# A query tile's projection moved from step 3 to step 2, and two bursts of value products placed later, in an attention kernel

## The reference

```python
xn = layer_norm(x, norm_w, norm_b)
q = (xn @ q_w + q_b).reshape(Bx, Tx, H, -1)
k = (xn @ k_w + k_b).reshape(Bx, Tx, H, -1)
att = jnp.einsum('bnhl,bmhl->bnmh', q, k)
att = jax.nn.softmax(att + (1.0 - mask) * -1000000.0, axis=2)
v = ((xn @ v_w + v_b) * src_mask[:, :, None]).reshape(Bx, Tx, H, -1)
y = jnp.einsum('bnmh,bmhl->bnhl', att, v).reshape(Bx, Tx, Dx)
```

## Time and profile before

| | us |
|---|---|
| median of three runs | 2839.5 (2839.39 to 2840.51) |
| the profiled execution | 2837.53 |
| its span, first to last instruction | 2835.7 |
| mean granted TensorE clock | 0.981 |

### The profile page before, as it was taken

How to read it: one execution, slowest core, us unless ns; L and a number is a source line. 1 busy time by engine, 2 the same in 40 slices (tenths; PEclk the granted TensorE clock), 3 DMA queues, 4 the chain that set the end, 5 groups by cost and what they waited for, 6 DMA issues and landing times. The chain is left out here.

```text
span 2835.7 us, 43874 instructions
## 1 busy us (share of the span) xinstructions
PE 2684.1 (95%) x13890; PEld 1951.8 (69%) x13890; DVE 1822.6 (64%) x3276; ACT 1228.2 (43%) x2040; POOL 1343.5 (47%) x598
## 2 busy tenths in 40 slices
PE   6899999999999999999999689999999999999997
PEld 3565566556655665566555468888888888888886
DVE  4666666666666666666665566777676677666673
ACT  2455555555555555555555423333333333333332
POOL 0365655655666565556566323433333333433332
PEclk9999999999999999999999799999999999999999
DMA  7555656665666566656654411111111111111100
GB/s 181 123 95 95 94 80 94 94 96 78 94 97 98 74 97 98 96 78 96 95 83 69 147 35 49 49 49 45 48 49 45 36 46 41 49 49 35 47 30 30
DMA packets 114915, 211.44 MB, mean 75 GB/s; under 512 B 12408, under 2 KB 14508, under 8 KB 114876
## 3 DMA queue, kind: packets, MB, share of 16 engines
q1 hardware_dynamic: 78012, 143.81, 21.7%
q10 hardware_dynamic: 36864, 67.13, 17.8%
HBM read 74.87 MB, written 34.18 MB: 38 GB/s over the span
## 5 line engine op out<-in xcount | busy, mean ns | idle before, releaser
L879 DVE TENSOR_REDUCE negmax<-max_bank 128x1 f32<-128x512 f32 x1024 | 684.5, 687 | 333.6 <-PE max_bank L506 329.4
L745 ACT ACTIVATE probs<-exp_bank 128x512 f32<-128x512 f32 x1024 | 591.9, 596 | 564.2 <-PE exp_bank L521 469.0
L284 POOL TENSOR_TENSOR probs_sum<-probs_sum,probs 128x2048 f32<-128x2048 f32 x126 | 580.6, 4608 | 86.2 <-ACT probs L745 83.8
L284 POOL TENSOR_TENSOR probs_sum<-probs 128x2048 f32<-128x2048 f32 x63 | 287.9, 4570 | 587.0 <-ACT probs L745 587.0
L506 PE MATMUL max_bank<-k_stack,q_stack 98*128 98x512 f32 x1024 | 426.6, 418 | 27.6 <-DVE negmax L879 22.8
L521 PE MATMUL exp_bank<-q_stack,k_stack 100*128 100x512 f32 x1024 | 422.5, 424 | 23.1 <-ACT probs L745 22.5
L506 PEld LDWEIGHTS max_bank<-k_stack,q_stack 98*128 98x128 f32 x1024 | 195.2, 191 | 149.0 <-issue 58.5
L521 PEld LDWEIGHTS exp_bank<-q_stack,k_stack 100*128 100x128 f32 x1024 | 193.6, 190 | 127.6 <-ACT probs L745 73.1
L1500 POOL TENSOR_TENSOR sT_lo<-silu,sT_hi 128x512 fp32r<-128x512 f32 x128 | 172.8, 1370 | 175.8 <-DVE sT_hi L1615 175.8
L532 PE MATMUL y_bank<-probs,v_sb 128*32 128x512 f32 x2048 | 247.7, 602 | 0.0
L1281 PE MATMUL b_work<-ident,area 128*128 128x128 f32 x1536 | 192.8, 281 | 23.8 <-DMA b_sums<-sums_scratch 12.0
(11 more groups left out here) (203 smaller groups left out, 5308.6 us busy)
## 6 DMA issues: line engine op xcount, KB each, us to landing
q_stack<-q_stage ACTq DMA_DIRECT2D x128, 256.0 KB
k_stack<-k_stage ACTq DMA_DIRECT2D x128, 256.0 KB
x_sb<-in_x SPq DMA_DIRECT2D x16, 1024.0 KB, 5.4
q_stack<-q_stage SPq DMA_DIRECT2D x64, 256.0 KB
k_stack<-k_stage SPq DMA_DIRECT2D x64, 256.0 KB
yT_scratch<-y_stage SPq DMA_DIRECT2D x64, 256.0 KB
area<-yT_scratch SPq DMA_DIRECT2D x16, 1024.0 KB, 5.3
area<-in_x SPq DMA_DIRECT2D x64, 256.0 KB, 2.8
```

The costliest lines, as they stand in the source:

```text
L284: eng.tensor_tensor(probs_sum[:, :, :], so_far, probs[:, mt, :, :], ALU.add).then_inc(probs_added, 1)
L745: act.activation(probs[:, mt, j, :], exp_bank[k % 2][:, :], ACT.Exp).then_inc(exp_done, 1)
L879: dve.tensor_reduce(negmax[:, m:m + 1], max_bank[m % 2][:, :], AXX, ALU.max, negate=True).then_inc(max_done, 1)
```

## The change

Four things are altered.

- The tables `QUARTERS` and the rules in `uses_of` become one table `TILES`: for each step, each tile, its group, and the slots of its quarters. The q tile of group 1 of the next row moves from step 3 (slots 0 to 3) to step 2 (named q', slots 8 to 11). The k tile of group 1 stays in step 3, with its quarters in slots 0, 2, 4, 6 in place of 4 to 7. The other tiles keep their slots.
- The first burst and ACT's copy of y stand with exponential 6 in place of 5 (slot 9), in all steps.
- The second burst stands with exponential 10 (slot 13) in steps 1 and 2; in steps 0 and 3 it stays with exponential 8.
- The semaphores of the stacks are kept apart for q and k, so that a wait for one does not count the copies of the other; SP's low part of q' stands behind the shift rows of step 2.

```diff
-        stack_in = [sem(f"stack_in{g}") for g in range(NG)]
+        stack_in = {n: [sem(f"{n}_stack_in{g}") for g in range(NG)] for n in "qk"}
...
+        def tiles_of(g, last):
+            return {n: t for n, t in TILES[g].items() if not last or g == 0 or (g == 1 and n in "qk")}
+
         def uses_of(g, last):
...
+            at = [(slots[0], n) for n, (_, slots) in tiles_of(g, last).items()]
             if g == 1 and not last:
+                at += [(k, f"x{tt}") for tt, k in enumerate(X_TURNS)]
             if not last or g < NG - 1:
+                at.append((MAX_TURN, "m"))
+            return [n for _, n in sorted(at)]
+
+        TILES = [
+            {"q": (2, (0, 1, 2, 3)), "k": (2, (4, 5, 6, 7)), "v2": (2, (8, 9, 10, 11)), "v3": (3, (13, 14, 15, 15))},
+            {"q": (3, (0, 1, 2, 3)), "k": (3, (4, 5, 6, 7))},
+            {"q": (0, (0, 1, 2, 3)), "k": (0, (4, 5, 6, 7)), "q'": (1, (8, 9, 10, 11))},
+            {"k": (1, (0, 2, 4, 6)), "v0": (0, (8, 9, 10, 11)), "v1": (1, (13, 14, 15, 15))},
+        ]
+        X_TURNS = (8, 9, 11, 13)
+        MAX_TURN = 12
+        SECOND_BURST = (8, 10, 10, 8)
...
-        QUARTERS = {"q": (0, 1, 2, 3), "k": (4, 5, 6, 7), "v": (8, 9, 10, 11), "v'": (13, 14, 15, 15)}
...
+        def stacked(b, g, name):
+            group = TILES[g][name][0]
+            return (b, group) if group > g else (b + 1, group)
+
+        def copied(n, b, g):
+            return (stack_in[n][g], DMA * STACK_DMAS[n] * (b + 1))
+
+        def group_in_front(b, g):
+            return (b, g - 1) if g else (b - 1, NG - 1)
+
+        STACK_DMAS = {"q": 3, "k": 3 + 1}
...
                     shift_rows(n_b, n_g, use(b, g, "m", last)[1] + 1)
+                if "q'" in tiles:
+                    low_in("q'")
...
                 if m == 0:
-                    pe.wait_ge(stack_in[g], DMA * STACK_DMAS * (b + 1))
+                    for n in "qk":
+                        pe.wait_ge(*copied(n, b, g))
...
                 before = (b, g - 1) if g else (b - 1, NG - 1)
-                if e == 5 and not first:
+                if e == 6 and not first:
                     weigh_values(*before, 2)
                     weigh_values(*before, 3)
                     sum_probs(*before)
-                if e == 8:
+                if e == SECOND_BURST[g]:
                     weigh_values(b, g, 0)
                     weigh_values(b, g, 1)
...
                 exp(b, g, e, first)
-                if e == 5 and not first:
+                if e == 6 and not first:
                     copy_y(*((b, g - 1) if g else (b - 1, NG - 1)))
...
+                    for name, (tile, slots) in tiles_of(g, last).items():
+                        if name[0] in "qk" and k == slots[-1]:
+                            act.wait_ge(*copied(name[0], *group_in_front(*stacked(b, g, name))))
+                            static, number = use(b, g, name, last)
+                            high_of(name[0], tile, number, static)
+                            stack_high(name[0], tile, high_count(b, g, name))
...
+                    for name, (tile, slots) in tiles_of(g, last).items():
+                        if name[0] in "qk" and k == slots[-1] + 1:
+                            low_of(name[0], tile, use(b, g, name, last)[0], high_count(b, g, name))
```

More of the change, by code:

```diff
@@ L366, in step, with low_in @@
             def step(b, g, last=False, first=False):
-                if not last or g < NG - 2:
-                    s_b, s_g = (b, g + 2) if g + 2 < NG else (b + 1, g + 2 - NG)
-                    if not (first and g + 2 < NG):
+                tiles = tiles_of(g, last)
+                if "k" in tiles:
+                    s_b, s_g = stacked(b, g, "k")
+                    if not (first and g < 2):
                         sp.wait_ge(exp_full, SLOTS * (step_of(b, g) - 1))
                     mask_rows(s_b, s_g)
[L373 to L379, removed]
+                def low_in(name):
+                    sp.wait_ge(work_read, use(b, g, name, last)[1] + 1)
+                    stack_low(name[0], stacked(b, g, name)[1])
+                for name in "qk":
+                    if name in tiles:
+                        low_in(name)
                 if not (first and g == 0):
@@ L684, in step @@
                             if kt == 0:
-                                banks[name] = take_bank(use(b, g, u, last))
-                            project_quarter(what, tile, banks[name], kt, kt == 0, kt == KT - 1)
+                                banks[name] = take_bank(use(b, g, name, last))
+                            project_quarter(name[0], tile, banks[name], kt, kt == 0, kt == KT - 1)
                     if g == 1 and not last and k in X_TURNS:
@@ L725, in stack_high @@
                 for row in HIGH_ROWS[what]:
-                    act.dma_start(stack_rows(what, row, g), stage[what][:, 0, :].bitcast(F32)).then_inc(stack_in[g], DMA)
+                    act.dma_start(stack_rows(what, row, g), stage[what][:, 0, :].bitcast(F32)).then_inc(stack_in[what][g], DMA)
             def mask_value(b, mt, number):
@@ L781, in _ @@
                     if g == 1:
-                        act.wait_ge(stack_in[0], DMA * STACK_DMAS)
+                        act.wait_ge(*copied(what, 0, 0))
                     high_of(what, g, n, n)
@@ L803, in step @@
                         exp_slot(*exp_of(b, g, k), first and g == 0)
-                    for what in "qk":
-                        if k == QUARTERS[what][-1] and (not last or g < NG - 2):
-                            p_b, p_g = (b, g + 1) if g + 1 < NG else (b + 1, 0)
-                            act.wait_ge(stack_in[p_g], DMA * STACK_DMAS * (p_b + 1))
-                            static, number = use(b, g, what, last)
-                            high_of(what, (g + 2) % NG, number, static)
-                            stack_high(what, (g + 2) % NG, high_count(b, g, "qk".index(what)))
+                    for name, (tile, slots) in tiles_of(g, last).items():
[4 more added lines that the diff above has]
+                            stack_high(name[0], tile, high_count(b, g, name))
                     if g == 1 and not last and k in X_TURNS:
@@ L1011, in step @@
                             maximum(n_b, n_g, m)
-                    for i, what in enumerate("qk"):
-                        if k == QUARTERS[what][-1] + 1 and (not last or g < NG - 2):
-                            low_of(what, (g + 2) % NG, use(b, g, what, last)[0], high_count(b, g, i))
+                    for name, (tile, slots) in tiles_of(g, last).items():
+                        if name[0] in "qk" and k == slots[-1] + 1:
+                            low_of(name[0], tile, use(b, g, name, last)[0], high_count(b, g, name))
                     if g == 1 and not last and 5 <= k < 5 + TT:
```

41 lines of the change are left out of this document (7 added, 34 removed).

## The result

| | before | after |
|---|---|---|
| median, us | 2839.56 (2839.39 to 2840.51) | 2890.02 (2887.53 to 2891.81) |
| span of the profiled execution, us | 2835.7 | 2889.0 |
| mean granted clock | 0.981 | 0.974 |

The ratio is 1.0176, with a 95% interval of 1.0159 to 1.0194: the kernel is 50 us slower. The forecast was 2834.8 us in a range of 2827 to 2849; the measured time lies 41 us above the range.

What follows compares the result with a forecast made beforehand. PE, busy 95%, was taken as the bound in slots with projections, with waits for VectorE and ScalarE elsewhere. Steps and last row summed to +4.3 us, the clock to -9.0: 2839.5 - 4.7 = 2834.8 us, range 2827 to 2849.

Steps and rivals of the forecast that it cites:

- rival B: Step 2: transfers and low part queued behind q' come late, costing 1 us more per row, 2850 us; chance 0.09.
- "nothing" for e0 of step 3: Exponential 0 of step 3 needs the shift rows at 15.3, they land by 13.5 to 14: no cost.
- step 2: With q' and the second burst behind exponential 10, ScalarE's stop is partly exposed: +1.18 us per row.
- the old falls: Clock falls at step 2's opening, seven of 1.5 us: 10.5 us go, one fall stays, -9.0 us.
- the last row: Row b = 15: -0.78 us in each of steps 1 and 2, some -0.4 at step 3's burst, -2.0 us together.
- Rival C: ScalarE's stops in steps 2 and 3 are hidden after all: some 0.5 us less per row, 2827 us; chance 0.13.
- Steps 0 and 3: First burst one exponential later in these steps: the same work in another order, cost 0.
- Step 3 without the wait: Step 3 with twelve matmuls fewer and k in slots 0, 2, 4, 6, paced by VectorE: -0.35 us per row.
- Step 1: Step 1 with both bursts later; waits for VectorE move to x2 and the maxima's transpose: -0.41 us per row.
- rival D: Step 1 gains nothing because VectorE's chain is longer than laid: +6 us, 2841 us; chance 0.09.
- rival A: Clock falls in step 1's second burst, 1.5 us each; nine to 14 falls give 2847 to 2854 us; chance 0.12.
- The Trainium skill: By its rule DMAs of different engines interleave; step 2's shift rows land near 12.3 and rival B is worth nothing.

Runs made afterwards that it cites:

- y_late: Kernel after, with SP issuing the 256 KB store of y behind the shift rows of step 2 instead of ahead; 2844.62 us, ratio 1.0024.
- filler: Kernel after, with eight unread projection-sized matmuls added on PE just ahead of exponential 0 of step 3; 2874.66 us, ratio 1.0126.
- e13: Not a run: exponential 13 of a step on PE, which by the lag of three opens the next step; steps are measured from one to the next.
- e5: Not a run: exponential 5 of a step on PE, in slot 8; the forecast counts its times within a step from it as zero.
- bursts_only: Kernel before, with both bursts moved (first to exponential 6, second to 10 in steps 1 and 2) and no tile moved; 2817.16 us, ratio 0.9922.
- e6: Not a run: exponential 6 of a step on PE, in slot 9; the change puts the first burst with it.
- norm_moved2: first_only with VectorE's normalising multiplies of slots 6 and 7 of step 1 moved to slot 8; 2814.58 us, ratio 0.9911.
- late_dma: Kernel after, with ScalarE issuing both copies of q' in slot 14, behind the shift rows; 2845.15 us, ratio 1.0021.
- first_only: Kernel before, with only the first burst and the copy of y moved, to exponential 6; 2813.55 us, ratio 0.9910.
- first_e7: first_only with the first burst and the copy of y one exponential later, at 7; 2855.61 us, ratio 1.0053 to the kernel before.

## Why the prediction was wrong, point by point

- **The step that failed is the landing of the shift rows** (rival B and, in the sum, "nothing" for e0 of step 3). I put them at 13.5 to 14 against a need at 15.3, from the stretch of the earlier trace rows in which two copies alone were through four microseconds after their issue. They landed at 17.13; the need was right (e0 of y_late stands at 15.43). Missing in that estimate was the load already under way: the store of y (issued at 4.2) runs into q', and y_late, where it is gone, measures 14.93. Even that is later than 13.5 to 14. I had named the mechanism, priced it at 1 us per row, and given it 0.09; it cost 1.89 (filler against y_late).
- **The clock that follows a wait was not in rival B at all.** The fall in step 3 costs another 1.16 us per row. The two together are 3.04 x 15 = 46 us of the 50, and y_late, without both, is some 45 us faster than the kernel after. The rest is step 2's +1.18 x 15 = +18, less 7 x 1.5 = 10.5 for the old falls and 2 for the last row.
- **Step 2: right.** 22.3 us against 22.28 predicted (21.1 + 1.18), with e13 at 11.63 after e5 (11.67 predicted), behind ScalarE's stop as laid out (high part at 937.19, next exponential over at 939.83, 2.64 us). Rival C, that such stops are hidden, did not come. Steps 0 and 3 lose nothing by the later first burst, as forecast (24.49 against 24.50; step 3 of bursts_only 24.60).
- **Step 3 without the wait: the waits are there, the gain is not.** Predicted -0.35, measured +0.04 (24.64 in y_late against 24.60). These twelve matmuls gave nothing back. PE stands before maxima 3, 6, 9 and 12, as predicted, and e6 waits for ScalarE's stop for k. Its timeline, y_late:

```profile
924.14 0.50 PE L524 MATMUL max_bank<-k_stack,q_stack 98*128 98x512 f32 x1 [0.32 <-DVE negmax L887]
925.75 0.49 PE L539 MATMUL exp_bank<-q_stack,k_stack 100*128 100x512 f32 x1 [0.39 <-ACT probs L754]
```

  e5 starts 9.37 us after e13 (9.22 predicted), e6 at 11.69 (11.41), and the slot with the burst takes 4.41 where the sum leaves 4.30, its length in bursts_only: 0.15, 0.13 and 0.11 us too little.
- **Step 1: -0.41 predicted, nothing measured** (22.94 against 22.91). The waits are where I put them, but I left one out. Timeline of PE, kernel after, from e5 of step 1:

```profile
906.34 0.39 PE L537 MATMUL exp_bank<-q_stack,k_stack 100*128 100x512 f32 x1
907.06 0.50 PE L522 MATMUL max_bank<-k_stack,q_stack 98*128 98x512 f32 x1 [0.33 <-DVE negmax L885]
...
913.44 0.66 PE L511 MATMUL work_bank<-ident,x_sb 128*128 128x128 f32 x4 [0.53 <-DVE xT_lo L866]
...
914.71 0.27 PE L528 MATMUL work_bank<-ident,negmax 128*16 128x128 f32 x1 [0.38 <-DVE xT_lo L866]
...
918.84 0.50 PE L537 MATMUL exp_bank<-q_stack,k_stack 100*128 100x512 f32 x1 [0.70 <-ACT probs L752]
```

  x2 and the maxima's transpose wait for VectorE as forecast. But maximum 12, which no longer has the burst ahead of it, waits as well: slot 8 takes 1.40 us where I laid 0.92. norm_moved2 shows whose queue that is: with the multiplies out of the way the slot takes 0.95. The forecast of rival D (step 1 gains nothing, at +6 us) came true beside the main loss.
- **The last row: the sum is right by luck.** -1.8 us against -2.0, but by its steps 20.1, 17.8 and 15.4 (20.9, 17.4 and 16.7 before): step 1 -0.8 as forecast, step 2 +0.4 in place of -0.78, step 3 -1.3 in place of -0.4, and there the stretch at the lower clock is 3.4 us long in place of 6.8, which no term of mine holds.
- **The old falls: right where they were, wrong in sum.** Not one at the opening of step 2 is left, and rival A's falls in step 1's second burst did not come. I took one fall for the whole kernel; there are 14 in step 3 of the rows b = 0 to 14, all with the wait.
- **The Trainium skill** (DMA: Bandwidth & Descriptors, section Issuing engines are not separate DMA queues) has DMAs of all issuers interleave on the same 16 engines. I had set it against the earlier trace rows and said that by it the shift rows land near 12.3. This trace shows both at work in part. The view of the queues, kernel after, 939.9 to 942.0, just after the shift rows' issue on SP (q1), and then 942.0 to 944.9:

```profile
q10 hardware_dynamic: 147, 0.27, 97.2%
q1 hardware_dynamic: 40, 0.07, 9.1%
```

```profile
q1 hardware_dynamic: 191, 0.26, 82.7%
q10 hardware_dynamic: 56, 0.08, 26.1%
```

  Packets of both queues move in either stretch, so the two do interleave, and half of the shift rows is down at 15.49, ahead of the second copy of q' (16.47). But the shares swing from one queue to the other, and the other half lands 0.7 us behind 512 KB that were issued before it. (0.07 and 0.26 MB of q1 are far more than 16 KB: SP's store of y, low part and load of x are in them, and the view doesn't tell the shift rows from these.) To read the rule as "a small copy is not held up" was wrong; the experiments decide, with 2.2 to 2.7 us per 256 KB for the second row.

What stays open: why the DMA engines served the two queues in these shares, and why, of ends of step 1 that look alike in the table by stretch, some bring a fall and others none. The counts of falls are of one profiled execution for each kernel.

## What to carry to other kernels

A move of work in time also moves its DMAs: before moving a tile, list every transfer that is in flight when the next small, urgent copy is issued (the store of another queue too), take their sum in bytes at the measured rate, and compare it with the slack of that copy; where it doesn't fit, send the bulk after the urgent copy, as y_late and late_dma do. Matmuls taken out of a step give nothing back if another engine paces its slots (step 3 here, 24.64 against 24.60 us with twelve fewer). And put a long burst where it covers the work of other engines that PE would wait for next: here the first burst belongs behind exponential 6, above VectorE's work on k, which at exponential 5 comes behind it, and no later, since ScalarE's stop for k must lie under it too. That alone is worth 0.9% (first_only), some 0.4% of it falls that stayed away without a reason shown.

## What the runs showed of the hardware

- A wait of 1.6 us of PE in a stretch that was otherwise loose came with the 1.2 GHz level (granted clock 0.50) for some 3.4 us, in three rows for twice as long; in the row where the wait was 0.79 us no fall came. With eight unread matmuls in place of the wait the clock stayed at 1.00 in b = 1 to 14, and the kernel took 15 us less.
- The granted clock isn't told by PE's share alone: 1.86 us of PE in 3.40 was followed by none (norm_moved2, b = 8), 2.05 in 3.60 by one (b = 9).
- A DMA of 8 KB (the second shift row) landed 1.85, 4.6 and 6.7 us after its issue with none, one and two 256 KB copies of another engine's queue ahead of it and a 256 KB store of its own queue issued some 6 us before; with the two copies and without that store it was 4.5 us (y_late).
- Issuing the two copies holds ScalarE for 1.21 us, with 1.35 us between its high part and its next exponential; whether this is free hangs on the burst that PE happens to have there (first_e7 against first_only: 42 us, falls included).
